# Second cross attention of a decoder kernel: four score banks, one value bank, turns and values six heads behind the scores

## The reference, cut to what matters

```python
def _L1_xattn_ref(key, query, mask, w_q, w_k, w_v, w_o):
    sqrt_d = jnp.sqrt(jnp.float32(D))            # D = 64, 16 heads
    q = jnp.einsum('blj,njd->bnld', query, w_q)
    k = jnp.einsum('blj,njd->bnld', key, w_k)
    v = jnp.einsum('blj,njd->bnld', key, w_v)
    score = jnp.einsum('bnid,bnkd->bnik', q, k) / sqrt_d
    m = mask[:, None]
    score = score * m + NEG * (1.0 - m)
    attn = jax.nn.softmax(score, axis=-1)
    out = jnp.einsum('bnij,bnjk->bnik', attn, v)
    out = jnp.einsum('bnlj,njk->blk', out, w_o)
    return out
...
    x = x + _L1_xattn_ref(ctx_1024, _layernorm(x, axis=-1), mask_BxSxS2_fk1, L1_xattn_w_q, ...)
```

## Time and profile before

| what | us |
|---|---|
| median of 3 runs (lowest to highest) | 1762.19 (1760.85 to 1763.37) |
| the profiled execution, its own time | 1767.52 |
| its span in the trace | 1765.8 |
| the second cross attention in it, first query projection to last add | 1385.03 to 1692.47 |
| PE busy over the whole span | 1315.4 (74%) |
| DVE busy over the whole span | 1426.4 (81%) |
| ACT busy over the whole span | 1101.4 (62%) |
| POOL busy over the whole span | 1140.0 (65%) |

### The profile page before, as it was taken

The page is one execution under the profiler, slowest core; times in us unless marked ns, Lnnn a source line. Parts: engine busy times, 40 slices in busy tenths (PEclk is TensorE's granted clock), DMA queues, the critical chain, the costliest instruction groups (busy, mean ns, idle before and its releaser), DMA issues. The chain is left out here.

```text
span 1765.8 us, 23296 instructions
## 1 busy us (share of the span) xinstructions
PE 1315.4 (74%) x6904; PEld 648.2 (37%) x6907; DVE 1426.4 (81%) x2430; ACT 1101.4 (62%) x2435; POOL 1140.0 (65%) x742
## 2 busy tenths in 40 slices
PE   6777898986757656767567666667746799899979
PEld 4554565553322212222122222212201465566543
DVE  4654898978259999999999999999996477777845
ACT  4444887876566566676566666566644577777740
POOL 2101565651079999999999999999994144444410
PEclk9999999998878888798888888888867799999989
DMA  3000000000054453353443443543332311111000
GB/s 102 1 1 2 1 2 1 1 20 7 6 223 164 190 191 133 132 207 138 191 186 145 145 186 137 198 186 145 121 136 80 111 49 49 48 72 72 1 1 24
DMA packets 70215, 168.03 MB, mean 95 GB/s; under 512 B 20420, under 2 KB 40152, under 8 KB 56664
## 3 DMA queue, kind: packets, MB, share of 16 engines
q1 hardware_dynamic: 68680, 166.17, 25.6%
q10 hardware_dynamic: 1168, 0.53, 0.1%
q0 software_dynamic: 256, 0.01, 0.0%
HBM read 131.04 MB, written 35.65 MB: 94 GB/s over the span
## 5 line engine op out<-in xcount | busy, mean ns | idle before, releaser
L1633 POOL TENSOR_TENSOR ma_hs<-ma_dtuR,ma_Bt 128x1024 f32<-128x1024 f32 x256 | 596.6, 2358 | 7.0 <-DMA ma_dtuR<-ma_dtu_d 6.7
L1816 ACT ACTIVATE ps<-ma_dtR,ma_A 128x512 f32<-128x512 f32 x512 | 332.7, 682 | 297.2 <-DVE ma_hs L1961 254.8
L845 POOL TENSOR_TENSOR x_pr<-x_pr,x_rec 128x512 f32<-128x512 f32 x256 | 267.4, 1045 | 291.6 <-DVE x_rec L1085 291.6
L1955 DVE TENSOR_TENSOR_SCAN ps<-ps,ma_hs 128x1024 f32<-128x1024 f32 x176 | 401.5, 2281 | 0.2
L1710 PE MATMUL ps<-ma_hs,ma_fold 128*32 128x512 f32 x1024 | 174.7, 816 | 206.1 <-POOL ma_hs L1641 177.4
L1051 ACT ACTIVATE x_pr<-x_sm,x_mx 128x256 f32<-128x256 f32 x512 | 255.2, 500 | 68.9 <-DVE x_mx L1076 65.9
L1961 DVE TENSOR_TENSOR ma_hs<-ps,ma_Ct 128x1024 f32<-128x1024 f32 x176 | 215.4, 1224 | 6.1
L1955 DVE TENSOR_TENSOR_SCAN ma_hs<-ps,ma_hs 128x1024 f32<-128x1024 f32 x80 | 182.5, 2281 | 18.3 <-ACT ps L1816 15.4
L1641 POOL TENSOR_TENSOR ma_hs<-ma_hs,ma_Ct 128x1024 f32<-128x1024 f32 x80 | 188.2, 2353 | 12.3 <-DVE ma_hs L1955 12.1
L1677 PE MATMUL ps<-ma_hn,ma_w_tap 128*128 128x512 f32 (+3 forms) x256 | 142.0, 707 | 52.4 <-ACT ma_hn L1840 52.4
L907 PE MATMUL ps<-ident,x_pr 128*128 128x128 f32 x1024 | 163.2, 286 | 5.4 <-DVE x_pT L985 4.4
(11 more groups left out here) (304 smaller groups left out, 2168.6 us busy)
## 6 DMA issues: line engine op xcount, KB each, us to landing
ma_dtuR<-ma_dtu_d SPq DMA_DIRECT2D x32, 1024.0 KB, 6.7
ma_dtR<-ma_dt_d SPq DMA_DIRECT2D x32, 1024.0 KB, 8.7
ma_Bt<-ma_bc_d SPq DMA_DIRECT2D x16, 1024.0 KB, 5.0
ma_Ct<-ma_bc_d SPq DMA_DIRECT2D x16, 1024.0 KB, 7.4
ma_dtu_d<-ma_dtu SPq DMA_DIRECT2D x32, 256.0 KB, 2.0
ma_dt_d<-ma_dt SPq DMA_DIRECT2D x32, 256.0 KB, 2.3
keys_d<-ma_kv SPq DMA_DIRECT2D x32, 256.0 KB, 4.4
values_d<-ma_kv SPq DMA_DIRECT2D x32, 256.0 KB, 2.5
```

The costliest lines, as they stand in the source:

```text
L845: pool.tensor_tensor(pr[:, r, :, :], pr[:, r, :, :], rec[:, r, :].unsqueeze(2).broadcast_to([P, 2, L]), ALU.mult).then_inc(pr_done, 1)
L1633: pool.tensor_tensor(hs[:, k % SLOTS, :, :], dtuR[:, unit(f, h), q, :].unsqueeze(1).broadcast_to([P, 2, CH]), rows(Bt, k), ALU.mult).then_ ...
L1816: e = act.activation(c.ps[:, 2 * (k % 2) + a, :], dtR[:, unit(f, h), q, :], ACT.Exp, scale=A[:, (f // QUARTERS) % 2, h, q, no:no + 1])
L1955: dve.tensor_tensor_scan(out, pair(k), slot(k), 0.0, ALU.mult, ALU.add).then_inc(scan_done, 1)
```

## The change

It sets new constants for x1 and moves its banks:

- Scores get four banks, (0, 1) and (5, 7), for pairs in turn; a bank is free for head n when head n-4 is masked, so PE waits for `s_free` of n-2 in place of n.
- `LAG` is 6, so turns and values stand six items behind the scores and not four; the output projection moves from item 7 to item 9, its add from item 8 to item 10.
- Query projections of the next batch stand one each in items 3, 4, 5 and 6, and all use bank 6. Each waits until ACT has taken out the one before; the output projection uses bank 6 too and waits until the four are taken out.
- Values use bank 4 alone. The first group of four heads waits until DVE has copied the four heads before; earlier it waited for those before that.

x0 keeps its banks, its lag and its order.

```diff
-    LAG = 4
+    LAG = 4 if small else 6
...
-    WO = 6 if small else 7
-    SCORE_BANKS = ((0, 1), (5, 7)) if small else ((0, 1),)
+    WO = 6
+    SCORE_BANKS = ((0, 1), (5, 7))
...
         def units(n):
 
-            a = n - FIRST_UNIT
-            if small:
-                return range(a - 1, a) if 1 <= a <= NP else range(0)
-            return range(min(NP, a * 3 // 2), min(NP, (a + 1) * 3 // 2)) if a >= 0 else range(0)
+            a = n - (FIRST_UNIT + 1 if small else 3)
+            return range(a, a + 1) if 0 <= a < NP else range(0)
...
-                    bank = c.ps[:, projection_bank(n), :]
-                    if small and n >= 1:
+                    bank = c.ps[:, WO, :]
+                    if n >= 1 or not first:
                         pe.wait_ge(evac, b * NP + n)
-                    elif n >= 2:
-                        pe.wait_ge(evac, b * NP + n - 1)
-                    elif not first:
-                        pe.wait_ge(evac, b * NP)
-                    if 6 + n == WO and not first and not second:
-                        pe.wait_ge(x_done, b - 1)
+                    if n == 0 and not first and not second:
+                        pe.wait_ge(x_done, b - 1 if small else b - 2)
...
-                    if small and (n >= 4 or not first):
-                        pe.wait_ge(max_done, b * NH + n - 2)
-                    elif not small and (n >= 2 or not first):
-                        pe.wait_ge(s_free, b * NH + n)
+                    if n >= 4 or not first:
+                        pe.wait_ge(max_done if small else s_free, b * NH + n - 2)
...
-                    if not small and g % 2 == 0 and (g >= 4 or not first):
-                        pe.wait_ge(oT_done, b * NO + g // 2 - 1)
+                    if not small and g % 2 == 0 and (g >= 2 or not first):
+                        pe.wait_ge(oT_done, b * NO + g // 2)
...
-                                mm = pe.matmul(c.ps[64 * r:64 * r + 64, O0 + h // 4 % 2, at:at + L],
+                                mm = pe.matmul(c.ps[64 * r:64 * r + 64, O0, at:at + L],
...
-                        pe.wait_ge(evac, b * NP + NP)
+                        pe.wait_ge(evac, b * NP + (NP if small else 2 * NP))
...
                         if n == 0 and not first and not second:
-                            act.wait_ge(pv, b * NG - NG)
+                            act.wait_ge(scores, b * NH - NH)
```

More of the change, by code:

```diff
@@ L810, in score_bank @@
         def score_bank(n):
-            return SCORE_BANKS[(n // 2) % len(SCORE_BANKS)][n % 2]
-        def projection_bank(n):
-            return 6 if small else 6 + n % 2
+            return SCORE_BANKS[(n // 2) % 2][n % 2]
         with nc.Block() as block:
@@ L967, in body @@
                             for a in units(n):
-                                project(b + 1, a, False, first)
+                                project(b + 1, a, False, first if small else fresh)
                         if n == LAG + 3 and not first:
-                            out_projection(b, fresh, False)
+                            out_projection(b, fresh, last and not small)
                         step(b, p, n, first)
@@ L1094, in output_bank @@
                         dve.tensor_copy(oT[:, 2 * u:2 * u + 2, :].rearrange("p g q -> p (g q)"),
-                                        c.ps[:, O0 + u % 2, :]).then_inc(oT_done, 1)
+                                        c.ps[:, O0, :]).then_inc(oT_done, 1)
                 def finish(b):
```

## The result

| kernel | median of timed runs, us (lowest to highest) | profiled execution, its own time |
|---|---|---|
| before | 1762.04 (5 runs) | 1767.52 (the one ahead of the prediction), 1761.37 (run again) |
| after | 1769.57 (1766.58 to 1771.85, 5 runs) | 1771.15 |
| after, timed again | 1768.36 (1765.22 to 1771.78, 11 runs), before beside it 1762.53 | 1768.36 |

The ratio after/before is 1.0036 [1.0023, 1.0049], and 1.003 [1.0019, 1.0041] the second time. By the medians the change costs 7.5 us the first time and 5.8 the second. The forecast was 1761.0, with a range from 1753 to 1766: it missed the sign and the range.

What follows compares the result with a forecast made beforehand. Without waits PE would bound a batch at 33.1 us, but ACT's copies and the one value bank hold it back. Loop -3.6, opening +1.9, batch 0 -2.4 and end +2.9 sum to -1.2: 1761.0 us, range 1753 to 1766.

Steps and rivals of the forecast that it cites:

- The opening: Before batch 0's first scores: one bank makes the four query projections run one by one, +1.9 us.
- The opening stays slow: Rival, batch 0's first items: the clock stays at its lower level, adding 2 us, 1763; chance 0.10.
- Batch 0's "-2.4" for the pairs that are ready: Batch 0: four banks have the score pairs of items 2 and 4 ready, cutting DVE's waits from 4.8 to 2.4 us.
- The loop: Batches 1 to 6: period 35.9 against 36.47 us, 0.6 less each, -3.6 in all.
- The walk's legs: One loop batch's binding waits: DVE's item 15 copy to head 10 24.5 us, then 11.36 to the next copy.
- ACT's copy order holds PE: Loop: ACT's copies, listed between exponentials, keep PE at most two heads ahead of DVE at even items, whatever the banks.
- the purpose of four banks: Rival, loop: PE really gets ahead, 3.3 us less a batch, 1744, or 1753 for half of it; chance 0.12.
- its 33.1: Loop: PE's work in one batch without any waiting, 33.1 us.
- The end: Last batch: last mask product to stage end takes 15.5 us in place of 12.61, +2.9.
- One value bank costs more: Rival, loop: waits at items 4 and 8 cost 1 us each, period 37.9, kernel 1773; chance 0.12.

Runs made afterwards that it cites:

- the one-wait edit: The kernel before, with the first batch's four query projections each waiting until the one before is taken out; median 1772.58 us, ratio 1.0051.
- The early mask: The changed kernel with DVE's mask instruction for the next batch ahead of its value-bank copy in item 15; median 1764.05 us, ratio 1.0003.
- Values eight behind: The changed kernel with values eight items behind the scores, turns still six, output projection in item 11; median 1770.44 us, ratio 1.0043.
- lag 4: The changed kernel with turns and values four items behind the scores and the output projection in item 8; median 1769.94 us, ratio 1.0031.

## Why the prediction was wrong

**The opening, the step that failed.** The prediction put its one-by-one projections at +1.9, by taking two of them at 2.77 and "two at full clock", 1.82. In five of seven traces of a one-by-one opening none was at the full clock (4 x 2.76 up to the scores), and in the other two only the first. Against an opening with two banks that starts at the same level this is +3.8 or +5.4, not +1.9. The first product then comes another 0.9 later, because the first scores still run at the lower clock, a term that the sum did not have. The sum for batch 0 was +1.9 - 2.4 = -0.5; measured were +3.0 (both traces starting at the lower clock) and +6.0 (both at the full clock). The forecast start of the scores, 1394.2, looked near after's 1395.14 only because that trace began at the full clock and before's did not. The rows at hand said that the four projections ran at 0.50; that this is a draw of the execution, which falls the other way in four of fourteen traces, one trace could not say. The 5.3 between that execution and the median were a sign, and it was not followed.

**"The opening stays slow"** was the rival with the right mechanism, at 2 us and a chance of 0.10. It was priced as an addition to the +1.9 and not from an opening that stays at the lower clock throughout; measured, undoing the serial opening gives 5.7 to 6.9 back, and doing it to before costs 10. Two pages of the Trainium skill were cited on this side. Perfetto Trace Analysis, Matmuls, says that independent groups should rotate through PSUM banks; for four short projections the runs agree, at 6 to 10 us. TensorE: Matmul & The Clock Gate, What's actually happening, says that the throttled state is the default and activity releases it; the 30.7 us of the one-wait edit agree. Both were weighed too lightly.

**Batch 0's "-2.4" for the pairs that are ready.** From the first product to the next mask, after takes 1429.95 - 1397.32 = 32.63, before run again 1421.52 - 1388.57 = 32.95: 0.3 less. Between the two traces that start at the lower clock it is 32.53 against 34.31, 1.8 less; but after with two score banks took 31.02, so this isn't the banks' gain. They gave nothing there that a run shows; the granted clock from 1395 to 1405 and from 1405 to 1412 was 0.67 and 0.55 in after, 0.82 and 1.00 in the other.

**The loop, -3.6 forecast, -1.7 measured** against before run again, whose six batches mean 36.41. The walk's legs came out: DVE's copy to head 10 took 1526.25 - 1501.48 = 24.77 (forecast 24.5), head 10 to the next copy 11.36 (11.36), DVE's waits 3.18 and 0.86 at the two heads named (3.3 and 1.0), PE's waits 2.7 (2 to 3). The 0.3 missing is the mask: by the earlier trace rows it takes 0.80 from start to start, but behind the copy it took 1.11, and item 2's wait behind it became 0.97 where 0.75 was worked out. The early mask removes it, and 0.3 more.

**"ACT's copy order holds PE"** was half right. Values eight behind showed that the value bank ties it almost as closely, and two score banks showed that the four are worth 0.6 a batch. That the purpose of four banks would bring only little held: no edit brought PE near its 33.1.

**The end, +2.9 forecast, +3.2 measured** (15.77 against 12.61; forecast 15.5). Right, for the reasons given; lag 4 restores 12.62.

**"One value bank costs more"** did not happen at that price: 0.2 a batch on before's order, and a period of 36.13 with it in the changed one.

The measured terms against the forecast of -3.6 + 1.9 - 2.4 + 2.9 = -1.2 are: with both openings starting at the full clock -1.7 + 5.4 + 0.9 - 0.3 + 3.4 = +7.7, at the lower one -1.8 + 3.8 + 0.9 - 1.8 + 3.5 = +4.6. The end came near its forecast and the loop gave half of its own. By the forecast these two nearly cancel; that the sum changes its sign comes from the opening and from the missing half of the loop.

What the projections' move was worth apart from the rest was not asked in the prediction, and it is the largest number of the study: 9.4 us by one edit of two lines. The change took the projections away from the output projection too, but put them one behind the other in items 3 to 6 and paid for it with the value bank and the lag; set apart in items 9 to 14 on before's banks and lag, they take 1.5 a batch from DVE's waits where the change took 0.9.

## What to carry to other kernels

Where a stage opens with a few short matmuls after TensorE was idle, keep at least two banks there even if the loop needs the bank: a 0.69 break behind each kept the clock down, and together they cost 6 to 10 us. Before adding banks, spread the work that has no fixed place over the items where TensorE waits; here it took two lines and gave more than any bank. And when the profiled execution is 5 us off the median, find out where before building a sum on its rows, and compare two openings only when both start at the same clock.

## What the runs showed of the hardware

- **The clock falls inside a busy loop.** With PE busy for 33.3 of a batch's 35.8, a wait of 1.77 was followed in four of six batches by a stretch from, for instance, 1466.00 to 1469.40 at 0.50, worth 1.9 us each; periods are then either 35.7 or 37.6. It isn't peculiar to the new order: in batch 4 of before's first trace PE stands 1.86 for a score bank behind the long mask shown below (0.98 in the second trace), the clock is at 0.70 from 1577 to 1581, and the batch takes 37.88 and not 36.37.
- **DVE's mask instruction and POOL's product delay one another.** Elsewhere the mask takes 0.43 and the product 1.04. In after, the product is there first and the mask ends 0.28 behind it, at 1502.95; with the early mask both start at 1499.73 and the product takes 1.32; in batch 4 of before's first trace it is the mask that waits:

```profile
1501.63 1.04 POOL L839 TENSOR_TENSOR x_pr<-x_pr,x_rec 128x512 f32<-128x512 f32 x1 [0.79 <-DVE x_rec L1073]
```

```profile
1499.73 1.32 POOL L839 TENSOR_TENSOR x_pr<-x_pr,x_rec 128x512 f32<-128x512 f32 x1 [0.79 <-DVE x_rec L1073]
```

```profile
1573.54 1.04 POOL L845 TENSOR_TENSOR x_pr<-x_pr,x_rec 128x512 f32<-128x512 f32 x1 [0.79 <-DVE x_rec L1085]
1573.55 1.31 DVE L1130 TENSOR_SCALAR x_neg<-x_m 128x512 f32 x1
```

  The mask ends 0.28 behind the product's end where it waits, and the product is 0.28 longer where it does. The Trainium skill, Trainium Architecture — The Big Picture, What this means for kernel authors, says that VectorE and GpSimd contend for one shared pair of ports and that this is an exclusive lock, not a split of bandwidth. The rows fit this. No run changed POOL's product alone.
- **One trace of an opening is one draw.** The same kernel took 42.83 and 38.71 for batch 0; the clock in its first 5 us was at the lower level in one and at the upper in the other, after the same 3.30 of idle PE. The changed kernel took 45.78 and 44.70. What lies outside the stage, which no edit touches, varied as well: 1452.6 to 1461.3 over the fourteen traces. Differences of a few us between whole executions need medians, and single traces are compared batch by batch.
